# Layer norm stages of a four-layer graph network, each block with a place of its own in VectorE's program

## What is computed

```python
x = _layernorm(x + _L0(x, adj, ...))   # adj @ (f * (adj @ (x W))) twice, relu between
x = _layernorm(x + _L1(x, adj, W))     # [x, adj @ x] @ W
x = _layernorm(x + _L2(x, adj, ...))   # below
x = _layernorm(x + _L3(x, adj, W, b))  # swish(adj @ (.) @ W + b) twice
```

```python
messages = node_features @ W_msg + b_msg
probs = sigmoid(q @ k.T / scale + gate_bias)          # q, k = messages W_q, messages W_k
aggregated = (probs * adj * adj) @ messages
updated = relu(concat([node_features, aggregated]) @ W_upd + b_upd)
out = (updated - mu) * rsqrt(var + 1e-5) * ln_gamma + ln_beta
```

## Time and profile before

| | |
|---|---|
| median of 3 runs | 1713.41 us (1713.12 to 1714.25) |
| span of the profiled execution | 1712.5 us, 0.9 below the median |
| TensorE busy | 1622.0 us (95%) |
| VectorE busy | 1280.4 us (75%) |
| ScalarE busy | 1103.1 us (64%) |
| mean granted TensorE clock | 0.987 |
| moved from and to memory | 490.76 MB, mean 287 GB/s |

### The profile page before, as it was taken

The page is one execution under the profiler, slowest core; times in us unless marked ns, Lnnn a source line. Parts: engine busy times, 40 slices in busy tenths (PEclk is TensorE's granted clock), DMA queues, the critical chain, the costliest instruction groups (busy, mean ns, idle before and its releaser), DMA issues. The chain is left out here.

```text
span 1712.5 us, 18888 instructions
## 1 busy us (share of the span) xinstructions
PE 1622.0 (95%) x7618; PEld 761.2 (44%) x7618; DVE 1280.4 (75%) x1423; ACT 1103.1 (64%) x757; POOL 11.3 (1%) x25
## 2 busy tenths in 40 slices
PE   7999999999999999999999999899998899999996
PEld 4444444444444444444444444343444344444442
DVE  6876546653766498649996898989899996455997
ACT  5766847674786586656666677676767666445663
POOL 2000000000000000000000000000000000000000
PEclk9999999999999999999999999999999999999998
DMA  9979789977999789978677364454545797665892
GB/s 365 412 299 398 297 360 391 369 292 323 368 400 412 268 303 414 385 273 316 249 289 276 123 216 164 161 197 162 185 170 211 285 377 287 239 243 194 343 334 113
DMA packets 68423, 490.76 MB, mean 287 GB/s; under 512 B 7824, under 2 KB 7984, under 8 KB 9328
## 3 DMA queue, kind: packets, MB, share of 16 engines
q1 hardware_dynamic: 67104, 485.00, 74.1%
q0 software_dynamic: 1088, 4.49, 0.7%
q10 hardware_dynamic: 144, 0.07, 0.0%
HBM read 420.32 MB, written 69.21 MB: 286 GB/s over the span
## 5 line engine op out<-in xcount | busy, mean ns | idle before, releaser
L903 DVE SCALAR_TENSOR_TENSOR a_lo<-a_ring,a_hi 128x2048 f16<-128x2048 f32 x332 | 752.1, 2288 | 306.6 <-ACT a_hi L709 306.5
L709 ACT ACTIVATE a_hi<-a_ring 128x2048 f16<-128x2048 f32 x332 | 629.4, 1906 | 337.0 <-PE spare L531 195.2
L531 PE MATMUL acc<-a_hi,y_hi 128*128 128x512 f16 x1584 | 478.0, 383 | 58.2 <-DVE a_lo L903 35.4
L531 PE MATMUL acc<-a_hi,y_lo 128*128 128x512 f16 x1584 | 477.9, 383 | 0.0
L531 PE MATMUL acc<-a_lo,y_hi 128*128 128x512 f16 x1584 | 477.2, 382 | 0.0
L531 PEld LDWEIGHTS acc<-a_hi,y_hi 128*128 128x128 f16 x1584 | 152.9, 98 | 254.0 <-DVE a_lo L903 43.4
L531 PEld LDWEIGHTS acc<-a_lo,y_hi 128*128 128x128 f16 x1584 | 155.6, 98 | 191.1 <-issue 6.6
L531 PEld LDWEIGHTS acc<-a_hi,y_lo 128*128 128x128 f16 x1584 | 155.6, 98 | 190.3 <-issue 5.3
L924 DVE SCALAR_TENSOR_TENSOR gates<-gates,a_ring 128x1024 f32<-128x1024 f32 x128 | 155.9, 1218 | 29.4 <-ACT gates L738 29.0
L721 ACT ACTIVATE a_hi<-gates 128x1024 f16<-128x1024 f32 x128 | 134.8, 1053 | 64.4 <-DVE gates L924 64.2
L911 DVE TENSOR_TENSOR a_lo<-gates,a_hi 128x1024 f16<-128x1024 f32 x128 | 155.8, 1217 | 0.0
(11 more groups left out here) (98 smaller groups left out, 671.9 us busy)
## 6 DMA issues: line engine op xcount, KB each, us to landing
a_ring<-adj_dram SPq DMA_DIRECT2D x332, 1024.0 KB, 7.4
saved_squares<-squares SPq DMA_DIRECT2D x64, 1024.0 KB, 12.3
a_ring<-saved_squares SPq DMA_DIRECT2D x64, 1024.0 KB, 4.8
x_T<-xt_dram SPq DMA_DIRECT2D x4, 512.0 KB, 8.1
x_rows<-x_dram POOLq DMA_DIRECT2D x1, 2048.0 KB, 12.1
out_dram<-x_rows POOLq DMA_DIRECT2D x3, 512.0 KB, 4.0
out_dram<-x_rows SPq DMA_DIRECT2D x2, 256.0 KB, 2.0
w<-W_dram POOLq DMA_DIRECT2D x2, 64.0 KB, 5.4
```

Source lines behind the costliest of these rows:

```text
L531: mm = pe.matmul(sums[:, h * BANK:(h + 1) * BANK], blk(y[:, y_pass % 2, :], j), slot(a, st)[:, s, h * BANK:(h + 1) * BANK], start=(begins ...
L709: act.activation(slot(a_hi, st), loaded(st), ACT.Copy, scale=2.0 ** A_EXP).then_inc(s_ahi, 1)
L903: dve.scalar_tensor_tensor(out=slot(a_lo, st).rearrange("p s c -> p (s c)"), in0=loaded(st).rearrange("p s c -> p (s c)"), scalar=2.0 ** A ...
```

## The change

The function with gamma and beta becomes two functions, and the lists of VectorE name one block per position. Positions on the other engines, and `LENGTH`, stay.

```diff
-            def normalise_affine(p, k):
+            def affine_gain(p, k):
 
                 n = nth("ln", p, k, 0)
                 dve.wait_ge(s_newton, 3 * NEWTON * n)
                 for b in range(CB):
                     dve.scalar_tensor_tensor(out=xn[:, b, :], in0=val[:, b, :], scalar=moments[:, b, 0:1], in1=gam[:, :],
                                              op0=ALU.subtract, op1=ALU.mult).then_inc(s_scaled, 1)
+
+            def affine_shift(p, k):
+
                 for b in range(CB):
                     dve.wait_ge(s_scaled, CB * (nth("resid", p, k) - 1) + b + 1)
...
-                4: {0: [take_over], 1: [values, ln_moments(0, s_val, "val"), ln_rstd(0), normalise(0)], 5: [y_low]},
-                5: {0: [take_over], 1: [values], 2: [ln_moments(0, s_val, "val"), ln_rstd(0), normalise(0)],
+                4: {0: [take_over], 1: [values], 2: [ln_moments(0, s_val, "val")], 3: [ln_rstd(0)], 4: [normalise(0)],
+                    5: [y_low]},
+                5: {0: [take_over], 1: [values], 2: [ln_moments(0, s_val, "val")], 3: [ln_rstd(0)], 4: [normalise(0)],
                     7: [qk_low(0, kT_hi, kT_lo, K_EXP)], 8: [qk_low(1, qT_hi, qT_lo, Q_EXP)], 9: [y_low]},
-                6: {5: [values], 8: [ln_moments(0, s_nl, "nonlin")], 10: [ln_rstd(0)], 12: [normalise_affine],
-                    15: [residual], 17: [ln_moments(1, s_res, "resid")], 20: [ln_rstd(1)], 21: [normalise(1)],
+                6: {5: [values], 8: [ln_moments(0, s_nl, "nonlin")], 10: [ln_rstd(0)], 12: [affine_gain],
+                    13: [affine_shift], 15: [residual], 17: [ln_moments(1, s_res, "resid")], 20: [ln_rstd(1)], 21: [normalise(1)],
...
-                8: {0: [take_over], 2: [swish], 4: [residual], 5: [ln_moments(0, s_res, "resid")], 6: [ln_rstd(0), normalise(0)]},
-                LAST_GATED: {2: [values], 4: [ln_moments(0, s_nl, "nonlin")], 5: [ln_rstd(0)], 6: [normalise_affine],
-                    8: [residual], 10: [ln_moments(1, s_res, "resid")], 11: [ln_rstd(1), normalise(1)], 14: [y_low]},
+                8: {0: [take_over], 2: [swish], 4: [residual], 5: [ln_moments(0, s_res, "resid")], 6: [ln_rstd(0)],
+                    7: [normalise(0)]},
+                LAST_GATED: {2: [values], 4: [ln_moments(0, s_nl, "nonlin")], 5: [ln_rstd(0)], 6: [affine_gain],
+                    7: [affine_shift], 8: [residual], 10: [ln_moments(1, s_res, "resid")], 11: [ln_rstd(1)],
+                    12: [normalise(1)], 14: [y_low]},
```

## The result

The changed kernel takes 1723.79 us (median of 4 runs, 1722.29 to 1726.74) against 1713.55 (4 runs): a ratio of 1.0059, 95% interval 1.0045 to 1.0072. The forecast was 1721.5, slower. The execution that was profiled spans 1720.5 us (1712.5 before).

A forecast was written before the change was run, and what follows sets the result against it. TensorE was taken as nearly never idle, with VectorE the late engine in layer norms. Terms +9.0 - 2.65 - 1.1 - 1.6 - 2.2 + 6.4, with +0.4, gave +8.3 us: forecast 1721.5 us, range 1714.5 to 1725.0.

The forecast's parts named there:

- Waits in pass 5, +3.0 a chunk: Pass 5 chunks 0 to 2: TensorE waits 4.28 us for the application before its transposes; +9.0 us for three chunks.
- Clock, +6.4 in four places at 1.6: Half clock behind four new stalls, three in pass 5, one at pass 4 chunk 1's take-over; ends 0 and +13.
- Pass 4 chunk 2, -2.65: Pass 4 chunk 2: the 2.49 us stall goes and the transposes are just not late; -2.65 us.
- Chunk 3 with the take-over, -1.1: Pass 4 chunk 3 to pass 5's opening take-over: only VectorE's own waits behind ScalarE's loads go; -1.1 us.
- Pass 4 chunk 0, 0 for the wait: Pass 4 chunk 0: the 3.42 us stall moves to the take-over, then about 4 us long; 0 for the wait.
- Pass 5 chunk 3, +0.4: Pass 5's fourth chunk: late transposes replace the 3.4 us gates stall, 0 (bounds -1, +1); half-clock transposes add +0.4 us.
- Gated chunks, 0: Gated chunks 0 to 2: the 2.90 us gain-and-shift stall breaks in two, VectorE finishes its backlog at the same time; 0.
- Gated chunk 3, -1.6: Last gated chunk, behind the second application: a unit starts at 1375.85, not 1377.47; -1.6 us.
- Pass 8, -2.2: Pass 8: three stalls of 2.58 us break into 0.65 and 1.8; -2.2 us together, bounds -3.5 and -1.0.
- Rival 1: The stalls just break up, no new wait in pass 5, the gains stay: -7.5 us, 1706; chance 0.08.
- The rule quoted with it: If Vector is unsaturated but causes bubbles elsewhere, breaking up its work may complete sooner; by it alone the time falls.
- Rival 2: The new waits come but the clock does not fall: +1.5 to +2 us, 1715; chance 0.12.

The follow-up runs named there:

- p5_as_before: The changed kernel with the list of pass 5 as it was (statistics, root, application in one place): 1707.0 us, ratio 0.9960.
- only_p5: The kernel before with the spread list in pass 5 alone: 1732.3 us, ratio 1.0104.
- one_split: The changed kernel with root and application of pass 5 together in position 3, one split ahead of the application: 1707.1 us, ratio 0.9959.
- warm_everywhere: The changed kernel with 18 unread matmuls ahead of all four pass 5 application waits and the take-over wait of pass 4 chunk 1: 1713.7 us, ratio 0.9992.
- only_gain_shift: The kernel before with gain and shift at positions 12 and 13 in chunks 0 to 2 of the gated pass: 1715.3 us, ratio 1.0005.
- only_last_places: The kernel before with only the last gated chunk's second layer norm and the layer norms of pass 8 spread: 1712.0 us, ratio 0.9980.
- only_pass4: The kernel before with the spread list in pass 4 alone: 1711.0 us, ratio 0.9974.
- per_chunk: The changed kernel with pass 4 chunk 0 and pass 5 chunks 0 to 2 unspread, pass 5 chunk 3 root and application at 3: 1706.7 us, ratio 0.9950.

## Why the prediction was right

The sign, the place and the mechanism are those of the prediction; how close the sum came is in part luck, as its errors stand against each other. Its terms, with the two profiles of the changed kernel (first, second) and what the experiments add:

- *Waits in pass 5, +3.0 a chunk.* The waits measure 3.90 us (forecast 4.28; 0.25 of it is what statistics and root win, which the forecast had not), and with the clock held up a chunk costs 2.8 to 3.0. Shown by removing it (p5_as_before), by making it alone (only_p5) and by halving it (one_split).
- *Clock, +6.4 in four places at 1.6.* In pass 5 it is 2.5, 1.3 and 1.5, then 1.7, 2.5 and 1.7; behind chunk 0 of pass 4 it is 0.9, then 2.5. Sum 6.2 and 8.4. That half clock can last twice as long was in the upper end only; in each of the two profiles it did so at one of the three chunks in question.
- *Pass 4 chunk 2, -2.65.* -2.7 and -2.7. *Chunk 3 with the take-over, -1.1.* -1.7 and -1.7: undersized by 0.6. From the add of chunk 3 to the take-over VectorE takes 34.42 us before (766.51 to 800.93) and 32.86 after (764.25 to 797.11). Of the 1.56 us, 1.0 are its two waits behind ScalarE, as forecast; 0.36 are add, statistics and root, 0.12 each, which now have a split behind them; 0.2 are not traced to anything.
- *Pass 4 chunk 0, 0 for the wait.* +0.1 with the clock held up (warm_everywhere).
- *Pass 5 chunk 3, +0.4.* +1.5 and +2.0. With full clock throughout it wins 2.6 (warm_everywhere), but 1.7 of that is half clock behind the wait for the sigmoid, which the profile of before has and that of warm_everywhere has not. The other 0.9 stands against a stall that had half clock behind it in the kernel before; at some 1.7 us for that, the wait itself costs +0.7 (an estimate from these differences), inside its bounds. What was mis-sized is the clock: half clock is there in the kernel before as well, and the changed one has 6.8 us of it where that one has 3.4.
- *Gated chunks, 0.* 0.0, and no difference with this edit alone. *Gated chunk 3, -1.6.* -1.4. *Pass 8, -2.2.* -2.4 and -2.3. TensorE's waits for splits from 1600 to 1700 us in the changed kernel are five, the longest 1.5 us, where three of 2.6 stood, and full clock follows:

```profile
PE acc L531 <- DVE a_lo L909: 5.6, 5, 1.5
```

The sum, +8.3, stands against +8.0 in the first profile and +11.5 in the second. The time came out 2.3 us above the forecast. Of that, part is the distance between span and time: I put the median 0.9 above the span, but the profiled execution of the changed kernel took 1722.29 us, 1.8 over its span of 1720.5, and the same distance puts the one before at 1714.25, the slowest of its first three, while the one after was the fastest of its four. Half clock that lasts longer in other executions is part of the rest: the second profile shows it for one, 3.4 us slower than the first, 2.2 of them in the four places of the clock's term. For the others it is not shown; the mean granted clocks of the first four executions (0.987 to 0.990) do not rank them, the slowest has 0.989.

Rival 1 is what happens without the line of pass 5: I gave it -7.5 us, and p5_as_before has 0.9960, -6.9. So near a match is luck too: its profile has +2.5 in chunk 0 of pass 4 and -1.7 in chunk 3 of pass 5, both by the clock and neither in the rival's sum. The rule quoted with it (the Trainium skill, Perfetto Trace Analysis, Optimizing Scalar/DVE Operations) speaks of breaking up instructions; here none is broken up, and groups of them are spread. Carried over to groups it holds for chunks 2 and 3 of pass 4 and for pass 8, where TensorE starts sooner, and is silent on the one thing that decided: whether a reader stands close behind the last piece. Rival 2 (waits without the clock) is the kernel warm_everywhere: 0.9992, or -1.4 us, where I had +1.5 to +2; what is missing is the 2.6 us in chunk 3 of pass 5, most of them clock, and the 0.6 by which chunk 3 of pass 4 was undersized.

The forecast named the stall of 2.90 us as one that keeps full clock. The same profile has two more of 2.91 us in the next gated chunks, with half clock behind both, so its list was more mixed than it says; for waits of 3.9 to 4.1 us it was right every time.

Open: the spread of 3 to 4 us from run to run. The kernel before has it too, and warm_everywhere keeps it. One source can be seen in the profiles: in some executions half clock also follows a wait of 2.36 us near 454 us, which makes the +1.4 to +1.9 of several columns at the head of the table. Others can be seen where an experiment has the code of before: half clock behind the stall of 2.5 us in chunk 2 of pass 4 in only_gain_shift, and behind the one in chunk 3 in only_last_places, 1.7 us each. The profile of the kernel before is one of the better ones in this respect (mean granted clock 0.987, against 0.981 to 0.987 in its executions beside the experiments). What else adds to the spread was not tried.

## What to carry to other kernels

Before a block is spread over later places of an in-order engine, look up for each of its results how long before its first reader it is done; where that is 0.1 us, as here, the reader's engine waits for all that is put ahead of the block, and gets back only the stall that stood behind the reader: two splits cost it 2.9 us at full clock, one split 0.8. The readers can be moved along, where the work behind them has room for it. Spreading pays where splits are late and no reader is near; it moves nothing where the engine is busy 99% of the stage, however much shorter the stalls look. Price a stall of TensorE with what the clock takes behind it: here 1.3 to 2.5 us on top of a wait that cost 2.9. And before a difference between two traces is put down to an edit, look whether it also comes between two executions of the same code: here 1.7 us at a time did.

## What had not been expected of the hardware

Half clock behind the same wait of 3.9 us lasts 3.4 us in one execution and 6.8 in another, and which chunk gets the longer one changes from one execution to the next, while all waits repeat to 0.1 us. All 21 waits of 3.90 to 4.12 us in the fourteen profiles had half clock behind them. Below that it is mixed: one of 3.42 us (only_gain_shift, at 640.64) and one of 3.64 (only_pass4, at 1347.36) kept full clock. The waits of 1.83 and 1.84 us in chunks 0 to 2 of one_split kept it too, and those of 1.96 and 1.97 in the last chunk of one_split and per_chunk had half clock behind them; one of 2.12 us for the sigmoid had it 9 times out of 15; one of 2.36 us near 454 us, which all kernels have, had half clock behind it in seven of fourteen profiles. So between 1.96 and 3.7 us the length of a single wait does not settle it.
